# Four weight turns of an attention + FFN layer move from behind attention into its last two slots

## The reference, cut to what matters

```python
q = (x @ wq.T + bq).reshape(B, S, H, D)          # B 4, S 512, H 32, D 16; k and v alike
scores = jnp.einsum('bshd,bstd->bsht', q, k) / np.sqrt(D)
context = jnp.einsum('bsht,bstd->bshd', softmax(scores), v).reshape(B, S, E)
x1 = layernorm(x + context)
gate = jnp.einsum('bsd,hd->bsh', x1, dq1)        # dq1, dq2: 1376 x 512, dq3: 512 x 1376
up = jnp.einsum('bsd,hd->bsh', x1, dq2)
out = layernorm(x1 + jnp.einsum('bsh,dh->bsd', silu(gate) * up, dq3))
```

## Time and profile before

| what | value |
|---|---|
| median of the timed runs | 748.9 us |
| the profiled execution's own time | 751.0 us |
| its span (first to last instruction) | 749.2 us |
| PE busy, DVE busy, ACT busy, POOL busy | 677.3, 596.2, 471.8, 108.6 us |
| mean granted TensorE clock | 0.953 |
| attention's slots (first to last scores) | 166.1 to 321.6 us |
| first matmul of the FFN | 346.46 us |

### The profile page before, as it was taken

One profiled execution on the slowest core, in us unless ns is written; L12 is line 12 of the kernel. 1 busy time (PEld: TensorE's weight loads), 2 busy tenths in 40 slices (PEclk: granted clock), 3 DMA queues, 4 the chain that ended last, 5 costly groups with the idle time before them and its releaser, 6 DMA issues.

```text
span 749.2 us, 14519 instructions
## 1 busy us (share of the span) xinstructions
PE 677.3 (90%) x5808; PEld 554.8 (74%) x5808; DVE 596.2 (80%) x820; ACT 471.8 (63%) x642; POOL 108.6 (14%) x98
## 2 busy tenths in 40 slices
PE   4989999998975969758999999999999999999983
PEld 4878878787864858647888788888887788888761
DVE  2379999889987998957978998998878995544386
ACT  3579989886736647358538788886557663332134
POOL 0104412151101010101101221111120201000022
PEclk9999999999997978879999999999999999999995
DMA  9744359864685776728034542013313101330437
GB/s 212 195 116 151 122 167 194 183 199 80 119 117 84 179 143 161 194 89 307 1 113 143 195 114 86 16 57 101 143 36 128 63 1 29 140 118 14 164 116 168
DMA packets 132850, 92.90 MB, mean 124 GB/s; under 512 B 90256, under 2 KB 111760, under 8 KB 131504
## 3 DMA queue, kind: packets, MB, share of 16 engines
q1 hardware_dynamic: 131648, 89.88, 44.4%
q10 hardware_dynamic: 1136, 2.10, 1.2%
HBM read 58.07 MB, written 33.88 MB: 123 GB/s over the span
## 4 chain that ended last, share of the span: by engine, by line
PE 57%; DVE 24%; issue 9%; ACT 6%; DMA 3%; POOL 1%; SPq 0%; DVEq 0%; POOLq 0%; ACTq 0%
DVE nf_acc L1190 11%; PE ps_s L952 9%; PE ps_s L954 9%; PE ps_s L953 8%; PE ps_p L952 8%; PE ps_p L953 8%; PE ps_p L954 8%; ACT nf_y L787 3%; PE ps_s L1035 2%; DVE prob L1219 2%; DVE smax L1215 2%; DMA part<-in_L_attn_hidden_states 1%; DVE y_tmp L1238 1%; PE ps_p L1061 1%; DVE st L1247 1%
## 5 line engine op out<-in xcount | busy, mean ns | idle before, releaser
L1190 DVE SCALAR_TENSOR_TENSOR nf_acc<-nf_y,nf_acc 128x1024 f32<-128x1024 f32 (+4 forms) x266 | 317.0, 1192 | 29.9 <-ACT nf_y L787 17.7
L787 ACT ACTIVATE nf_y<-nf_w,bound_b 128x1024 f32<-128x1024 f32 (+4 forms) x285 | 286.8, 1048 | 4.6 <-DVE nf_acc L1190 3.8
L707 POOL TENSOR_TENSOR nf_w<-nf_w,nf_rec 128x1024 f32<-128x1024 f32 (+4 forms) x19 | 44.4, 2334 | 306.3 <-DVE nf_rec L1174 306.3
L1324 DVE TENSOR_TENSOR silu<-silu,ps_s 128x512 f32<-128x512 f32 (+1 forms) x44 | 30.1, 684 | 68.1 <-PE ps_s L954 68.0
L952 PE MATMUL ps_p<-x_hl,w_hl 128*128 128x512 f32 x192 | 77.9, 406 | 5.3 <-DVE x_hl L1208 2.4
L952 PE MATMUL ps_s<-x_hl,f_ha 128*128 128x512 f32 x192 | 74.9, 390 | 1.7 <-DVE f_la L1208 1.7
L953 PE MATMUL ps_p<-x_hl,w_hl 128*128 128x512 f32 x192 | 76.0, 396 | 0.0
L934 ACT ACTIVATE hid_hl<-silu 128x512 fp32r<-128x512 f32 (+1 forms) x44 | 27.8, 632 | 76.4 <-DVE silu L1324 76.4
L954 PE MATMUL ps_p<-x_hl,w_hl 128*128 128x512 f32 x192 | 75.9, 395 | 0.0
L954 PE MATMUL ps_s<-x_hl,f_la 128*128 128x512 f32 x192 | 74.8, 390 | 0.0
L953 PE MATMUL ps_s<-x_hl,f_ha 128*128 128x512 f32 x192 | 74.8, 389 | 0.0
(11 more groups left out here) (106 smaller groups left out, 1183.2 us busy)
## 6 DMA issues: line engine op xcount, KB each, us to landing
x_hl<-x_parts SPq DMA_DIRECT2D x10, 2048.0 KB, 8.2
queries_keys<-qk_p SPq DMA_DIRECT2D x32, 256.0 KB, 3.1
x_parts<-x_st SPq DMA_DIRECT2D x16, 512.0 KB, 3.6
nf_w<-in_L_ffn_w SPq DMA_DIRECT2D x24, 256.0 KB, 3.1
dequantised<-nf_acc SPq DMA_DIRECT2D x10, 512.0 KB, 2.8
v_blocks<-v_t SPq DMA_DIRECT2D x16, 256.0 KB, 4.0
k_st<-queries_keys SPq DMA_DIRECT2D x64, 64.0 KB, 3.9
v_bd<-v_blocks SPq DMA_DIRECT2D x32, 128.0 KB, 3.5
```

The costliest lines, as they stand in the source:

```text
L707: pool.tensor_tensor(v, v, nf_rec[0:p, 0:w // QBLOCK].unsqueeze(2).to_broadcast([p, w // QBLOCK, QBLOCK]), ALU.mult).then_inc(s_nnorm, 1)
L787: act.activation(nf_y[0:p, at % NY, 0:w], nf_w[0:p, u % 2, 0:w], ACT.Identity, bias=bound_b[0:p, i:i + 1], scale=STEEP).then_inc(s_ny, 1)
L1190: dve.scalar_tensor_tensor(out=acc, in0=y, scalar=float(NF4[i + 1]), in1=acc, op0=ALU.min, op1=ALU.max).then_inc(s_nacc, 1)
L1324: dve.tensor_tensor(h, h, ps_s[0:rows, 1], ALU.mult).then_inc(s_hid, 1)
```

## The change

The high rooms swap places: `f3_ha` and `hid_hl` (together as large as `f1_ha`) go where attention's keys lie, `f1_ha` goes behind attention's last room, with 1088 bytes of filler ahead of it. The highs of w1 and w2 then need no wait for the last scores; those of w3 keep it. The turns, highs and lows of w unit 0 move from `TAIL_1` to the end of slot 30, those of w unit 1 from `TAIL_2` to the end of slot 31 (behind x1 parts 0 and 1). `TAIL_1` and `TAIL_2` are then the two turns of w3 unit 0 and of w3 unit 1. The reloads of w units 0 and 1 move from slot 28 to slot 24 (GG - 2 NG), ahead of that slot's two stores of x1. No instruction is added or taken away.

```diff
+    W_AT = {GG - 2 + n: [("f", W_UNITS[n], s) for s in range(2)] for n in range(2)}
+    for G in range(GG + 1):
+        TURNS += CT_AT.get(G, []) + XT_AT.get(G, []) + W_AT.get(G, [])
-    TAIL_1 = [("f", u, s) for u in (W_UNITS[0], T_UNITS[0]) for s in range(2)]
-    TAIL_2 = [("f", u, s) for u in (T_UNITS[1], W_UNITS[1]) for s in range(2)]
+    TAIL_1, TAIL_2 = ([("f", u, s) for s in range(2)] for u in T_UNITS)
...
-    TAIL_S = (TAIL_1 + TAIL_2)[2:6]
+    TAIL_S = TAIL_1 + TAIL_2
...
         x1_hl1 = sb("x1_hl1", [P, 2, KC, BK], F32R)
-        f1_ha = sb("f1_ha", [P, 2, KC, NJG * P], F32R)
+        f3_ha = sb("f3_ha", [P, NJG, E], F32R)
+        hid_hl = sb("hid_hl", [P, 2, 2, BK], F32R)
...
-        hid_hl = sb("hid_hl", [P, 2, 2, BK], F32R)
...
-        f3_ha = sb("f3_ha", [P, NJG, E], F32R)
+        behind = sb("behind", [P, 1088 // 4], F32)
+        f1_ha = sb("f1_ha", [P, 2, KC, NJG * P], F32R)
...
+                if G == GG - 2 * NG:
+                    for u in W_UNITS[:2]:
+                        reload(u)
                 if G == GG - NG:
-                    for u in T_UNITS + W_UNITS:
+                    for u in T_UNITS + W_UNITS[2:]:
                         reload(u)
...
                     if g == 0:
-                        act.wait_ge(s_score, GG)
+                        if kind == "t":
+                            act.wait_ge(s_score, GG)
...
-                for key in XT_AT.get(G, []):
+                for key in XT_AT.get(G, []) + W_AT.get(G, []):
                     high(key)          # ACT; the same edit for turn(key) of TensorE and low(key) of DVE
```

More of the change, by code:

```diff
@@ L182, in layer_kernel @@
         BACK_AT.setdefault(G + 4 if G % 8 == 2 and G > 8 else G + 3, []).append(G)
-    for G in range(GG + 1):
-        TURNS += CT_AT.get(G, []) + XT_AT.get(G, [])
     T_UNITS = [u for u in range(NU0) if UNITS[u][0] == "t"]
     W_UNITS = [u for u in range(NU0) if UNITS[u][0] == "w"]
-    TAIL_1 = [("f", u, s) for u in (W_UNITS[0], T_UNITS[0]) for s in range(2)]
-    TAIL_2 = [("f", u, s) for u in (T_UNITS[1], W_UNITS[1]) for s in range(2)]
+    W_AT = {GG - 2 + n: [("f", W_UNITS[n], s) for s in range(2)] for n in range(2)}
+    for G in range(GG + 1):
+        TURNS += CT_AT.get(G, []) + XT_AT.get(G, []) + W_AT.get(G, [])
+    TAIL_1, TAIL_2 = ([("f", u, s) for s in range(2)] for u in T_UNITS)
     TURNS += TAIL_1 + TAIL_2
@@ L805, in high @@
                     dst = dst[0]
-                    g = UNITS[k][1]
+                    kind, g, _ = UNITS[k]
                     if g == 0:
-                        act.wait_ge(s_score, GG)
+                        if kind == "t":
+                            act.wait_ge(s_score, GG)
                     elif g == 1:
```

## The result

The changed kernel takes 753.49 us (median of 4 runs, 752.03 to 753.71), the kernel before 749.07 (4 runs, 748.63 to 749.6). The ratio is 1.0059, 95% interval 1.0043 to 1.0075: it is slower by 4.4 us where 2.1 faster was forecast. The profiled execution took 753.71 us, its span is 751.9 (before 751.0 and 749.2).

What follows compares the result with a forecast made beforehand. TensorE, busy 677 of 749 us, bounds the kernel, so its FFN must start earlier. The start gains 2.46 us (ACT's +1.0 included), less 0.35 for the clock: 748.9 - 2.1 = 746.8; range 745.9 to 749.8.

Steps and rivals of the forecast that it cites:

- the 2.46: Start of the FFN: first matmul 2.46 us earlier, at 344.0 instead of 346.46, all of it reaching the end.
- the part-by-part list: Costs of reloads and moved turns, highs and lows: all taken as 0 except +1.0 us on ACT in slot 30.
- the low that was to release the FFN: Low of w3 unit 1 on DVE: the FFN's first matmul waits for it and may start at 344.0.
- forecast 1.0: Slot 30 on ACT: two highs of w unit 0 ahead of norm_1 delay the path by 1.0 us, bounds 0.9 to 1.2.
- DVE's idle time: Ahead of slot 31's lift: 1.82 us idle cover the 1.2 us of w unit 0's two lows, cost 0.
- Held by something else: Rival, chance 0.09: x1 block 0's load lands 0.8 to 2.5 us later than set; gain 0 to 1.5, time 748.2.
- The 9.8: Load of x1 block 0 ahead of the FFN: 9.8 us from issue to landing, so landed at 343.2.
- the 0.8 us of slack: Between x1 block 0's landing at 343.2 and the FFN's first matmul at 344.0: 0.8 us left.
- Half clock: Rival, chance 0.18: the FFN starts at the low clock after TensorE idles; loss 1.5 us, gain 0.6, time 748.3.
- The rival that forecast a slower kernel: Rival, chance 0.12: slot 24's reloads delay slot 25's keys and scores(28); at keys landing 308, costs 4.2 us, time 751.0.
- the 3.7 us of slack: Slot 28: keys land about 300.1, scores may start at 303.8; 3.7 us exceed the reloads' 3.4, cost 0.
- the 5.2 us: Slot 28, upper bound of the reloads' cost: the keys land at 309 behind the extra megabyte on the DMA engines.

Runs made afterwards that it cites:

- e2: The kernel before with the changed kernel's rooms (1088 bytes of filler) and nothing of its schedule; 752.73 us, ratio 1.0048.
- e6: The kernel before with 64 bytes of filler ahead of all rooms of projection, attention and FFN; 748.74 us, ratio 1.0006.
- e9: The kernel before with 1088 bytes of filler ahead of f1_la, moving only the low rooms f1_la and f3_la; 751.20 us, ratio 1.0044.
- e11: The kernel before with 448 bytes of filler behind the projection's room, ahead of w_hl and x_hl_1; 748.03 us, ratio 0.9996.
- e1: The changed kernel with 2048 instead of 1088 bytes of filler ahead of f1_ha; 748.70 us, ratio 0.9992.
- e3: The changed kernel with 1536 instead of 1088 bytes of filler ahead of f1_ha; 746.56 us, ratio 0.9972.
- e7: The changed kernel with 1152 instead of 1088 bytes of filler; 752.06 us in one run.
- e8: The changed kernel with 1344 instead of 1088 bytes of filler; 752.21 us in one run.
- e12: The changed kernel with 2048 bytes of filler and 12 idle transposes behind back(30), load of x1 block 0 not moved; 748.65 us, ratio 1.0005.
- e4: The changed kernel with 2048 bytes of filler and the load of x1 block 0 issued in slot 30; 746.77 us, ratio 0.9968.
- e10: e4 plus 448 bytes of filler behind the projection's room, ahead of w_hl and x_hl_1; 746.79 us, ratio 0.9973.
- e5: e4 plus 12 transposes of the identity, result unread, behind back(30); 746.28 us, ratio 0.9976.

## Why the prediction was wrong

**The step that failed** is the sentence "In the FFN nothing else changes, and TensorE is the bound there, so the 2.46 should reach the end". The diff moves rooms, and the part-by-part list costs the reloads, turns, highs and lows but has no entry for the rooms at all. They were the largest term: +3.8 us (e2), by a matmul start every 233.4 instead of 226.9 ns, where the weights are in f1_ha or f1_la. That alone turns the forecast gain of 2.1 into a loss, and it puts the time beyond the stated range. The row that prices it was in the trace of before (projection blocks 2 and 3), and the arithmetic on the layout (1088 = 2 times 512 and 64) in the diff.

**The start** was right in mechanism up to the low that was to release the FFN, and wrong behind it. Slot 28 did not suffer from the reloads in slot 24: its scores did wait for the keys (the last landed at 300.76), but 1.02 us only (the view names the releaser "issue"), and ended 1.2 us ahead of DVE's `highest` at 304.17. That row of the changed kernel's TensorE timeline:

```profile
300.86 2.07 PE L1041 MATMUL ps_s<-k_st,q_st 32*32 32x64 f32 x64 [1.02 <-issue]
```

The two early highs of slot 30 put 0.95 us on ACT's path (forecast 1.0): x1 part 1's store is issued 26.80 behind the mark, before 25.85. The lows of w unit 0 found DVE's idle time. The timelines of ACT and of DVE after; the second DVE row is the low of w3 unit 1 which answers to 345.72 in the earlier trace rows:

```profile
321.25 1.07 ACT L819 ACTIVATE f_ha<-ps_t 128x512 fp32r<-128x512 f32 x2
322.21 2.92 ACT L868 ACTIVATE part<-part,nmr,rstd 128x512 f32<-128x512 f32 x4
```

```profile
321.87 1.29 DVE L1214 TENSOR_TENSOR f_la<-ps_t,f_ha 128x512 fp32r<-128x512 f32 x2 [0.20 <-ACT f_ha L819]
...
341.34 1.28 DVE L1214 TENSOR_TENSOR f_la<-ps_s,f_ha 128x512 fp32r<-128x512 f32 x2
```

That low (the first of the two in the row) was out 37.85 us behind the mark instead of 40.40, 2.55 earlier (forecast 2.46). Then both rivals for the start came true in the profile.

"Held by something else": the load of block 0 took 11.05 us, not 9.8, and cost 0.7. The 9.8 was one reading, and a lucky one: in the other traces with the old schedule (e2, e6, e9, e11) the same load takes 9.8 to 11.1 us, so the 0.8 us of slack was never safe.

"Half clock": 12 matmuls at 0.43 us instead of 0.23, about 2.4 us, more than the 1.5 priced, because the low clock lasted for 5.2 us where I had taken 3 from the earlier trace rows. The Trainium skill's rule ("TensorE: Matmul & The Clock Gate", part 1), that the array is throttled by default and activity releases it, agrees with this trace: 0.61 granted over 341 to 343 and 0.50 over 343 to 348, behind 1.2 busy us in 3. It was no accident of one execution, as all the traces together show:

| traces | first matmul behind the mark, us | clock over step 0 | step 1 behind the mark, us |
|---|---|---|---|
| old schedule: before, e2, e6, e9, e11 | 40.55 to 40.72 | 1.00 | 47.33 to 47.62 |
| early turns: changed, e1, e3, e7, e8 | 38.23 to 38.61 | 0.71 to 0.80 | 46.66 to 48.00 |
| early turns and transposes: e12 | 38.39 | 1.00 | 45.18 |
| early turns and early load: e4, e10 | 37.12, 37.90 | 1.00, 0.80 | 43.91, 46.29 |
| all three: e5 | 36.99 | 1.00 | 43.77 |

So the early turns brought the first matmul forward by about 2 us in all five traces, and half clock over step 0 (8.4 to 9.4 us long instead of 6.8) took 1.6 us or more of it each time. In e10 the early load did not keep the clock up either. The prediction gave this rival 0.18 and a gain of 0.6 that would be left. What stays open is its price in the median: filling the pause (e5, e12) moved no median.

**The rival that forecast a slower kernel** had its sign right by luck: it looked for the loss at the keys of slot 28. They did land 2.4 us later against the mark than before, but of the 3.7 us of slack that leaves 1.3; nothing of the 5.2 us came.

**What the moved turns are worth** with the rooms in step: the medians do not settle it. e1 (ratio 0.9992, 0.9978 to 1.0006) and e3 (0.9972, 0.9953 to 0.9992) differ by 512 bytes of filler alone and have the same start every 227 ns; they say 0.2 and 2.4 us, and e1's interval takes in no gain at all. With the rooms out of step the changed kernel (ratio 1.0059) is no faster than e2 (1.0048), which has the old schedule; their intervals overlap. The traces, read from the mark on, are closer together: to the end it is 443.1 to 443.3 us with the old schedule (before, e6, e11) and 442.8 in e1 and e3, so 0.4 us are won, where 2.1 were forecast. That is what half clock left of the start's 2 us. With the load early as well it is 439.8 (e4), 439.5 (e5) and 442.0 (e10, at half clock).

The best versions, e4 and e10, take 746.8 us, 0.3% under the kernel before; e3 and e5 cannot be told from them.

## What to carry to other kernels

A change of layout is a change of cost: for every operand that moves, work out its new distance from the operand it is multiplied with, and look for two groups of the same line in the trace that already differ in that. When a chain ahead of a long engine-bound stretch is shortened, look at once at what else releases its first instruction (here a load issued one store too late) and move that too. One profile shows where time goes in one execution; a gain of 1 us seen there needs a dozen runs before it is called one. Where executions scatter ahead of the stretch that was changed, compare the traces from a mark just ahead of it: here the mark lies anywhere from 302.7 to 306.1 us into the span, and from it to the end three traces with the same schedule and rooms in step (before, e6, e11) agree within 0.15 us.

## What the runs showed of the hardware

On this chip a 128 x 512 f32r matmul follows the one before after 227 ns at full clock if its weights and its moving data begin at the same place modulo 512 bytes of a partition, and after 233 ns at distances of 64, 128 and 320 (before, e1, e3 and e6 against the changed kernel, e2, e7 and e8); the loading of f_ha's weights itself takes 188 ns either way. Moving both by 64 bytes (e6) changes nothing. In a product of three matmuls, weights out of step slow their own matmul most (234.4) and the two others a little (229.6, e9). Behind a pause of 2.8 to 3.6 us of TensorE ahead of the FFN the granted clock over step 0 was 0.71 to 0.80 in six traces and 1.00 in one (e4); with 1.6 to 1.9 us (old schedule, e5, e12) it was 1.00 in all seven. The pause's length alone does not tell it: e4 idled for 2.97 us and kept its clock, e10 for 2.76 and did not.
